# Local attention: queries turned ahead of keys in one step of four, and VectorE copies the turned probabilities in another

## The reference, cut to what matters

```python
def attn_layer(x, Wqkv, qs, ksc, Wo):
    q, k, v = (sh(t) for t in jnp.split(x @ Wqkv, 3, -1))
    q = l2norm(q) * qs
    k = l2norm(k) * ksc
    q = q * cos * scale + rotate_half(q) * sin * scale
    k = k * cos * inv + rotate_half(k) * sin * inv
    out = local_attention(q, k, v)        # softmax over own window and the one before
    return out.transpose(0, 2, 1, 3).reshape(b, n, INNER) @ Wo

def ffn_layer(x, g, bln, W1, b1, W2, b2):
    xn = (x - mu) / jnp.sqrt(var + 1e-05) * g + bln
    a, gate = jnp.split(xn @ W1 + b1, 2, -1)
    return a * jax.nn.gelu(gate, approximate=False) @ W2 + b2

for i in range(DEPTH):                    # 6
    x = attn_layer(shift_tokens(x), ...) + x
    x = ffn_layer(shift_tokens(x), ...) + x
```

## Time and profile before

| | |
|---|---|
| median of 3 runs | 3920.93 us (3918.47 to 3923.31) |
| the profiled execution, its own time | 3922.12 us |
| its span | 3920.3 us |
| mean granted TensorE clock | 0.935 of full speed |
| busy: PE, PEld, DVE, ACT, POOL | 88%, 54%, 76%, 62%, 35% of the span |
| the stage of the change | from 1481 to 3253 us of the span |
| one round of four steps in it | 71.6 us, of it PE busy 69.0, DVE 58.9, ACT 51.7, POOL 47.9 |

### The profile page before, as it was taken

How to read it: one execution, slowest core, us unless ns; L and a number is a source line. 1 busy time by engine, 2 the same in 40 slices (tenths; PEclk the granted TensorE clock), 3 DMA queues, 4 the chain that set the end, 5 groups by cost and what they waited for, 6 DMA issues and landing times. The chain is left out here.

```text
span 3920.3 us, 103011 instructions
## 1 busy us (share of the span) xinstructions
PE 3430.9 (88%) x40985; PEld 2120.8 (54%) x40985; DVE 2976.8 (76%) x5754; ACT 2440.9 (62%) x4654; POOL 1382.0 (35%) x641
## 2 busy tenths in 40 slices
PE   5669668888859977999999999999999986998998
PEld 3347533333337844666666666666666653222785
DVE  6957757777738967888788888888888855887685
ACT  3436537777737845777767677677677752555572
POOL 3820011111100005676676676676676630000000
PEclk8879869999978988999999999999999996999899
DMA  1000047777601002322322322322322211100000
GB/s 42 0 8 5 14 159 232 234 230 230 220 12 65 17 1 50 102 65 60 100 60 66 97 63 60 100 62 61 102 61 62 60 41 60 37 25 13 14 16 11
DMA packets 174808, 285.79 MB, mean 73 GB/s; under 512 B 36980, under 2 KB 76917, under 8 KB 172405
## 3 DMA queue, kind: packets, MB, share of 16 engines
q1 hardware_dynamic: 173748, 278.48, 24.4%
q10 hardware_dynamic: 576, 0.69, 0.0%
HBM read 104.05 MB, written 74.45 MB: 46 GB/s over the span
## 5 line engine op out<-in xcount | busy, mean ns | idle before, releaser
L2304 POOL TENSOR_TENSOR b2f_norm<-b2f_norm,b2f_minus_half 128x16 f32<-128x16 f32 x192 | 555.1, 2910 | 292.7 <-DVE b2f_norm L2650 292.7
L2294 POOL TENSOR_TENSOR b2f_q<-b2f_q,b2f_q_part 128x1024 f32<-128x1024 f32 x96 | 228.2, 2377 | 588.0 <-DVE b2f_q_part L2640 588.0
L1725 ACT ACTIVATE b1a_weights<-b1a_b_ps 128x512 f32<-128x512 f32 x512 | 277.2, 596 | 39.7 <-PE b1a_b_ps L1650 37.2
L1840 DVE TENSOR_REDUCE b1a_tops<-b1a_a_ps 128x1 f32<-128x512 f32 (+3 forms) x512 | 244.6, 502 | 19.5 <-PE b1a_a_ps L1606 17.9
L1557 POOL TENSOR_SCALAR b1a_k_op<-b1a_k_op,b1a_extra 128x1024 bf16<-128x1024 bf16 x32 | 90.7, 2846 | 446.7 <-DMA b1a_k_op<-part_copies 408.9
L1725 ACT ACTIVATE b3a_weights<-b3a_b_ps 128x512 f32<-128x512 f32 (+3 forms) x384 | 161.3, 502 | 137.1 <-PE b3a_b_ps L1660 135.9
L2649 DVE TENSOR_REDUCE b2f_norm<-xn 128x16 f32<-128x1024 f32 x192 | 234.2, 1220 | 13.4 <-ACT xn L2530 5.7
L2592 ACT ACTIVATE b2f_v_rows<-b2f_q_ps 128x1024 f32<-128x1024 f32 x96 | 98.4, 1025 | 232.5 <-PE b2f_q_ps L2366 232.5
L2539 ACT ACTIVATE b2f_prob<-b2f_even_ps,b2f_bias,b2f_norm 128x64 f32<-128x64 f32 x768 | 232.6, 451 | 2.3 <-DVE b2f_bias L2666 2.3
L2539 ACT ACTIVATE b2f_prob<-b2f_odd_ps,b2f_bias,b2f_norm 128x64 f32<-128x64 f32 x768 | 232.6, 446 | 0.3
L1733 ACT ACTIVATE b1a_e_sb<-b1a_e_ps 128x512 f32<-128x512 f32 x256 | 153.1, 598 | 122.2 <-PE b1a_e_ps L1592 119.4
(11 more groups left out here) (519 smaller groups left out, 9183.6 us busy)
## 6 DMA issues: line engine op xcount, KB each, us to landing
b2f_values<-b2f_v_rows SPq DMA_DIRECT2D x1534, 64.0 KB
position_scratch<-b1a_e_sb SPq DMA_DIRECT2D x128, 512.0 KB, 4.0
b1a_band<-position_scratch SPq DMA_DIRECT2D x128, 384.0 KB
b2f_wqkv<-in_b2f_wqkv SPq DMA_DIRECT2D x6, 1536.0 KB, 7.4
b2f_turn<-in_c_rotary SPq DMA_DIRECT2D x6, 1024.0 KB, 8.5
b1f_raw<-in_b1f_both SPq DMA_DIRECT2D x9, 512.0 KB, 3.6
part_copies<-b1a_parts SPq DMA_DIRECT2D x12, 256.0 KB
b2f_wo<-in_b2f_wo SPq DMA_DIRECT2D x6, 512.0 KB, 9.5
```

The lines of the kernel that those rows point to most:

```text
L1725: act.activation(weights[:, s % P_RING, c, lo:QW], b_room(s, c)[:, lo:QW], ACT.Exp).then_inc(S.exps_ready, 1)
L1840: ins = dve.tensor_reduce(out, src, AX_X, ALU.max)
L2294: pool.tensor_tensor(G.q[:, g % 2], G.q[:, g % 2], G.q_part[:], ALU.add) \
L2304: pool.tensor_tensor(part, part, G.minus_half[:, 0:HEADS], ALU.pow) \
```

## The change

Two parts, each by a test of the step's phases:

1. In the step behind the gates TensorE turns the queries before the keys, and ScalarE copies them in that order. Elsewhere keys come first, as before.
2. In the gates' step the turned probabilities are copied by VectorE, between `store_tile` and `lengths`. ScalarE's copy is left out there. In the other steps ScalarE copies them, as before.

```diff
+    def has_phase(s, phase):
+        return any(at == phase for f, at in feed_forward(s))
...
+            def turn_keys(s, ps):
+                pe.wait_ge(S.k_normed, s)
+                if s >= 2:
+                    pe.wait_ge(S.exps_done, HEADS * (s - 1))
+                turn_rows(G.k[:, (s - 1) % 2], ps, S.kt_turned)
...
                 if 0 <= s - 1 < n_tiles:
-                    pe.wait_ge(S.k_normed, s)
-                    if s >= 2:
-                        pe.wait_ge(S.exps_done, HEADS * (s - 1))
-                    turn_rows(G.k[:, (s - 1) % 2], other, S.kt_turned)
+                    if not has_phase(s, 4):
+                        turn_keys(s, other)
                     pe.wait_ge(S.q_added, s)
                     turn_rows(G.q[:, (s - 1) % 2], here, S.qt_turned,
                               (lambda half: pe.wait_ge(S.o_copied, 2 * (s - 3) + half + 1))
                               if s >= 3 else None)
+                    if has_phase(s, 4):
+                        turn_keys(s, other)
...
+            def copy_keys(s, ps):
+                act.wait_ge(S.kt_turned, s)
+                if s >= 2:
+                    act.wait_ge(S.carried, s - 1)
+                act.activation(G.kt[:, :, WIN:], pairs(ps), ACT.Copy).then_inc(S.kt_copied, 1)
...
                 if 0 <= s - 1 < n_tiles:
-                    act.wait_ge(S.kt_turned, s)
-                    if s >= 2:
-                        act.wait_ge(S.carried, s - 1)
-                    act.activation(G.kt[:, :, WIN:], pairs(other), ACT.Copy).then_inc(S.kt_copied, 1)
+                    if not has_phase(s, 4):
+                        copy_keys(s, other)
                     act.wait_ge(S.qt_turned, s)
                     act.activation(G.qt[:], pairs(here), ACT.Copy).then_inc(S.qt_copied, 1)
+                    if has_phase(s, 4):
+                        copy_keys(s, other)
                 if s < n_tiles:
                     square(s, 1)
-                if 0 <= s - 2 < n_tiles:
+                if 0 <= s - 2 < n_tiles and not has_phase(s, 3):
                     act.wait_ge(S.probs_turned, s - 1)
...
+            def copy_turned(s, ps):
+                dve.wait_ge(S.probs_turned, s - 1)
+                if s >= 3:
+                    dve.wait_ge(S.out_ready, s - 2)
+                dve.tensor_copy(G.pt[:], ps[:].rearrange("p j (c n) -> p (j c) n", n=P)) \
+                    .then_inc(S.pt_copied, 1)
...
                 if 0 <= s - 3 < n_tiles:
                     store_tile(s - 3)
+                if 0 <= s - 2 < n_tiles and has_phase(s, 3):
+                    copy_turned(s, other)
                 if s < n_tiles:
                     lengths(s)
```

## The result

| | before | after |
|---|---|---|
| median of 18 runs each | 3919.21 us (3914.56 to 3923.32) | 3930.30 us (3922.51 to 3937.84) |
| ratio | | 1.0028, 95% interval 1.002 to 1.0035 |
| span of the profiled execution | 3920.3 us | 3923.8 us |

The change is slower by 11.1 us, between 7.8 and 13.7. The forecast was 11.0.

The account below looks back on a forecast made before the run. TensorE's work plus its remaining waits was taken to bound the steady part. Queries first, 22 x 0.50 = 11.0 us, plus 0 for the probabilities' copy, on 3920.93, gave 3932.0 us; range 3924 to 3939.

Parts of the forecast that it names:

- What bounds the stage: Steady part: a step lasts as long as TensorE's work plus its remaining waits, busy 1487.9 of 1549.0 us.
- Part 1, which wait stands first: Step behind the gates: queries wait for ScalarE's output-row copies, behind the exponentials, so TensorE waits about 1.4 us.
- Part 1, its size: Step behind the gates: TensorE falls behind by 0.50 us in each of 22 steps, +11.0 us.
- my low bound of 8.4: Least loss from queries first, without the modelled ends: 0.38 us late a step, 8.4 us in all.
- The five late steps: In 5 of 22 steps behind the gates TensorE arrives late by itself; these also lose 0.50 us each.
- Part 2: Gates' step, 23 steps: probabilities' copy moves from ScalarE to VectorE; waits on both engines absorb it, 0 us.
- give the loss back: Rival: the 0.50 us delay falls into a later TensorE wait; half back 3926 us, all 3921; chance 0.14.
- The relief of ScalarE: Rival: exponentials start earlier by ScalarE's lost copy, 23 x 1.02 us, giving 3908 us; chance 0.05.
- the rule of relieving the engine that TensorE waits for: Skill's rule: relieve the engine blocking the critical path; by it ScalarE's lost copy returns 23.5 us.
- VectorE's cover: Rival: VectorE's 1.44 us delay outlasts its waits before the next rotation, giving 3943 us; chance 0.07 together with a clock fall.
- The clock of the steady part: Rival: longer TensorE waits drop the clock to 0.83, giving 3969 us; chance 0.07 together with VectorE's lateness.

Follow-up runs that it names:

- Part 1 alone: Queries ahead of keys in the step behind the gates, ScalarE still copying turned probabilities everywhere, against the kernel before: 3927.91 against 3919.95 us, ratio 1.0022.
- part 2 alone: VectorE copies the turned probabilities in the gates' step, keys stay ahead of queries, against the kernel before: 3919.09 against 3919.95 us, ratio 0.9997.

## Why the prediction was right

*What bounds the stage.* Right. Part 1 alone and part 2 alone moved the time by what TensorE's order and waits say, 8.0 us against 22 x 0.36 and nothing against nothing. Queries first everywhere moved it the same way and by more than that, 46.8 us against 34.

*Part 1, which wait stands first.* Right in kind. The queries can't fill the wait for the exponentials, since ScalarE copies the output rows behind them; the row "1.60 <-ACT b2f_o_cols" stands where I put one of about 1.4. Moving those copies to VectorE took the loss away, and putting the queries first in other steps made it again.

*Part 1, its size.* The term was too large: 0.50 us forecast, 0.36 measured in a step. The queries' and keys' ends were right: keys done at 2370.00 + 1.04 = 2371.04, 2.58 behind, and I had 2369.48 - 2366.89 = 2.59. What I got wrong is the output projection, which I let start 0.50 later and last as long. It started 0.46 later and lasted 1.95 us instead of 2.05. So 22 x 0.36 = 7.9 us, below my low bound of 8.4, which had left out that the projection gets shorter; the first part alone measured 8.0. That the whole came out at 11.1, on the forecast, is luck as far as the steps tell: they account for 7.9, its interval holds 8.0 too, and where the other 3 us come from, if they are there, is open.

*The five late steps.* Right that they lose what the others lose, and mis-sized like them: 5.54 us against 5.18 is 0.36, not 0.50. The wait there is 0.78 us, all of it new.

*Part 2.* Right on both engines. ScalarE's wait ahead of the values became 2.19 (I had 1.92), and the first Gelu still waits 0.58 for its product. VectorE's copy takes 1.23; its delay is used up before the rotation, 0.47 left (I had 0.35). The copy of the probabilities alone costs nothing: 0.9997.

*The rivals.* Nothing is seen to give the loss back: the step behind the gates keeps its 0.36, and the other steps are as long as before. The relief of ScalarE, the rule of relieving the engine that TensorE waits for, fell: relieved before a wait, it only waited longer. VectorE's cover held here, and did not hold in the kernels that put two copies on it in every step or in three of four. The clock of the steady part stayed at 1.00, with 17 waits of 1.60 us in it.

## What to carry to other kernels

Before work is put into a wait, look at what frees its inputs: if that stands on the same engine *behind* what the wait is for, the work is later still. An engine that is late for another is helped by a smaller load only from its last own wait on; a copy taken away ahead of that wait became idle time here, 2.19 us instead of 0.90. And a gain of some tenths of a us in each step was lost again here to the engine that took over the work, so read its next waits before counting steps.

## What I had not expected

The output projection was shorter where nothing held it up. Before the change its weight loads and its products started together at 2368.84, just behind the end of ScalarE's square (2367.65 + 1.14 = 2368.79):

```profile
2368.84 1.86 PEld L2381 LDWEIGHTS b2f_q_ps<-b2f_o_cols,b2f_wo 128*128 128x128 f32 x16
```

With the change the square was done at 2370.35, and the loads started 0.11 us ahead of the first product (2370.87):

```profile
2370.76 1.87 PEld L2392 LDWEIGHTS b2f_q_ps<-b2f_o_cols,b2f_wo 128*128 128x128 f32 x16
```

The group became 0.10 us shorter, and this is the larger part of what my sum missed. It isn't only the modelled end that says so: the second product started 0.21 us behind the first one before, and starts 0.11 behind it now. The Trainium skill (Perfetto Trace Analysis, Tensor Engine Instruction) says that TensorE can pull weight loads ahead of products that are still under way. These rows agree: the load of 2370.76 runs beside the last key transpose, which is under way until 2371.04. Before the change the loads came no earlier than the products, since the group itself had just been waiting for the square.
